# A graph network's first loop: who adds a group's sums to the node table

## The chip, the cores and the metric

The kernel runs on one core of a Trainium2 chip. The metric is the device time of one execution in microseconds. Several runs are made of a kernel and their median is taken.

## The reference, cut to what matters

A graph has 3125 nodes with 64 features and 103125 directed edges (50000 drawn, the same reversed, one loop per node), sorted by destination. Two blocks work on it, each behind a layer norm and a relu, each with a residual. The first (`_L0_gnn_ref`) is two hyperbolic layers on the same graph; the second is a mean over edges of a two-layer perceptron. The part that this change touches is the sum over edges:

```
def hyp_agg(x, src, dst, w, c, n_nodes):
    xt = logmap0(x, c)
    msg = xt[src] * w[:, None]
    agg = jax.ops.segment_sum(msg, dst, num_segments=n_nodes)
    return proj(expmap0(agg, c), c)
```

It is run twice with the same `src`, `dst` and `w`, each time on another `xt`.

## The kernel before, in words

The edges are cut into `NG` = 48 groups of 17 x 128 = 2176. Because they are sorted by destination, the destinations of a group lie in a window of `W` = 72 consecutive nodes; a small table in SBUF (`tabi`) holds where each window begins, and `window(eng, g)` loads that number into a register of the engine that asks.

The first loop builds, for each group, a block matrix of edge weights (source node by destination in the window, 25 blocks of 125 x 72), stores it for the second layer, and applies it to the node table `A` at once. The engines run the loop side by side, each with its own program of bodies, and are tied by counting semaphores (`nth(i)` is the count behind step `i`).

- VectorE (`first_layer`, body for group g): `rank_edges(g+1)` (L1027, reads a PSUM bank), `bucket_edges(g+2)` (L1009), `edge_fields(g+1)` (L1018), `rank_onehots(g+1)` (L1032), `slot_destinations(g)` (L1040), `slot_sources(g)` (L1047), `slot_weights(g)` (three operations, L1055), and from the third body on `add_sums(g-2)` (L1066): it reads the window's place, waits for `applied` and adds the 128 x 72 sums in the bank `agg_ps` to the window of the table `aggTw`. The last two groups are added behind the loop, one on each side of the last apply.
- TensorE (`first_body`): `prefix(g+2)` (L1395 to L1398), `fill_slots(g+1)` (L1407), `first_apply(g-1)` (L1436, 50 small products into `agg_ps`), `slot_rows(g+1)` (L1427), `blocks(g)` (L1419, 75 products in four chunks). `first_apply` waits for the eviction of the block matrix and for `added` of the group before, since there is one bank `agg_ps`.
- ScalarE (`evict`): `third_weights(g)` (L653, 18 operations, waits for `dst1_set` of L1040), `take_slots(g+1)` (L639, L641, L642), `take_rows(g+1)` (L659), and the eviction of the four chunks of blocks (L670).
- SyncE stores the block matrix and the slot rows of each group.
- GpSimd does nothing in this loop. At the head it prepares constants and divides the source indices (L541 to L549) and clears `aggTw`; between the layers it clears two tables; in the last loop (`sum_messages` and its helpers) it subtracts 128 x 512 tiles (L595) beside VectorE.

Behind the loop VectorE waits for the last `added`, answers whether all ranks fit (`answer_ranks`), and folds the table (`act_scales`).

Of the kernel before, what the change touches and what calls it, by code (L numbers as in the profile page):

```python
# [16 lines left out]
NG = -(-E // GE)  # L17
# [43 lines left out]
def gnn_kernel(nc, x, src_t, dst_t, w_t, w0T, b0, w1T, b1, W1, eb1, W2, eb2, out):  # L61
# [5 lines left out]
    with ctx:  # L67
# [72 lines left out]
        def carve(words, dt=f32, parts=128):  # L140
            at[0] += words
            assert at[0] <= ARENA, at[0]
            view = arena[0:parts, at[0] - words:at[0]]
            return view if dt == f32 else view.bitcast(dt)
# [21 lines left out]
        slot_of = carve(NS * GTP // 2, bf16).rearrange("p (s t) -> p s t", t=GTP)  # L166
        minus = carve(64, bf16)[0:1, :]
        third = [carve(NB) for _ in range(2)]
        at[0] = 0
        PQ = carve(NB * HID)[0:PN].rearrange("p (b h) -> p b h", h=HID)  # L170
        P3 = carve(NB * 3 * HID // 2, bf16, PN).rearrange("p (b c h) -> p b c h", c=3, h=HID)
# [90 lines left out]
        def counts(name, n=1):  # L262

            made = [sem(f"{name}{i}") for i in range(n)]
            loop_sems.extend(made)
            return made if n > 1 else made[0]

        def nth(i):

            return i + 1 + PRIMED  # L270
# [5 lines left out]
                                "slots_set"))  # L276
        dst1_set, onehots_set, third_set = counts("dst1_set"), counts("onehots_set"), counts("third_set")
        blocks_done, blocks_set = (counts(n, len(CHUNKS)) for n in ("blocks_done", "blocks_set"))
        applied, added = counts("applied"), counts("added")
        saved = counts("saved")  # L280
        a_stored = sem("a_stored")

# [80 lines left out]
        def in_order(eng, stage):  # L363

            eng.wait_ge(table_set if stage == 0 else ranks_checked, 1)
            return eng.value_load(oki[0:1, stage:stage + 1], min_val=0, max_val=1)
# [145 lines left out]
        def _(pool):  # L512
# [45 lines left out]
            def any_gather(i, table, dest):  # L558
                with pool.Fori(0, NG) as g:
# [7 lines left out]
                    if i == 2:  # L567
                        pool.wait_ge(any_qidx[i], nth(g))
                        pool.sem_inc(begun, 1)
                        for t in range(GT):  # L570
                            pool.indirect_dma_start(GP[1][:, t, :], None, qf_d[:, :],
                                                    bass.IndirectOffsetOnAxis(ap=idx[1][:, t:t + 1], axis=0))\
                                .then_inc(any_gathered_q[i], 16)

            fast = in_order(pool, 1)
            for l in range(2):
                if l == 1:
# [30 lines left out]
        def _(sc):  # L608
# [27 lines left out]
            def take_slots(g, k):  # L636
                sc.wait_ge(slots_done, nth(g))
                sc.wait_ge(onehots_set, nth(g - 2))
                nc.scalar.activation(slot_dst[:, bass.ds(g, 1), :, :].rearrange("p g b d -> p (g b) d"),  # L639
                                     slots_ps[:, 1, 0:NB].unsqueeze(2).broadcast_to([128, NB, 2]), ACT.Copy)  # L640
                nc.scalar.activation(third[k], slots_ps[:, 4, 0:NB], ACT.Copy)  # L641
                nc.scalar.activation(slots[k][:, :, :, :].rearrange("p f b d -> p (f b) d"),  # L642
                                     slots_ps.rearrange("p f b -> p (f b)").unsqueeze(2)
                                     .broadcast_to([128, FIELDS * EB, 2]), ACT.Copy).then_inc(slots_set, 1)
# [11 lines left out]
            def take_rows(g, k):  # L656
                sc.wait_ge(row_done, nth(g))
                sc.wait_ge(row_saved, nth(g - 2))
                nc.scalar.activation(slot_row[k][:, :], row_t_ps, ACT.Copy).then_inc(row_set, 1)  # L659

            def evict(g, k, n):

                third_weights(g, k)
                take_slots(g + 1, 1 - k)
                take_rows(g + 1, 1 - k)
                sc.wait_ge(saved, nth(g - 2))
                sc.wait_ge(applied, nth(g - 2))
                for c, bs in enumerate(CHUNKS):
                    sc.wait_ge(blocks_done[c], nth(g))
                    nc.scalar.activation(AB[k][:, bs[0]:bs[-1] + 1, :], blocks_ps[c], ACT.Copy)\  # L670
                        .then_inc(blocks_set[c], 1)
# [27 lines left out]
            for l in range(2):  # L699
                sc.wait_ge(mu_ps, l + 1)  # L700
                for b in PIECES:
                    square(B[:, b, :], MU[:, b, :])
                answer_tanh()
                answer(ACT.Sqrt)
                answer(ACT.Ln)
                if l == 0:
                    sc.wait_ge(primed, 1)
                    fast = in_order(sc, 0)
                    with sc.If(fast == 1):
                        take_slots(0, 0)  # L710
                        take_rows(0, 0)
                        groups(sc, evict)
                    fast = in_order(sc, 1)

                if l == 0:
                    for c in range(len(QUADS)):
                        sc.wait_ge(fold_set, c + 1)
                        nc.scalar.activation(HT[0:F, QUADS[c][0]:QUADS[c][-1] + 1, :], quad_of(aggTw[0:F, :], c),
                                             ACT.Relu).then_inc(ht_set, 1)
                if l == 1:  # L720
                    square(B[:, :, :], sums_ps[l])
                if l == 1:
                    nc.scalar.activation(C[:, :, :], sums_ps[l], ACT.Relu).then_inc(relu_squared, 1)
                    sc.wait_ge(relu_squared, 1)
                    nc.scalar.activation(C[:, :, :], C[:, :, :], ACT.Square).then_inc(relu_squared, 1)
                answer(ACT.Sqrt)
                if l == 1:
                    answer_tanh()
# [61 lines left out]
        def _(ve):  # L790
# [267 lines left out]
                        slots[k][:, 2 + c, 0:n, :].unsqueeze(2).broadcast_to([128, n, HW, 2]), ALU.mult)  # L1058
                last.then_inc(onehots_set, 1)

            def add_sums(g):
                base = window(ve, g)
                ve.wait_ge(applied, nth(g))
                ve.wait_ge(added, nth(g - 1))
                win = aggTw[:, bass.ds(base, W)]
                nc.vector.tensor_tensor(win, win, agg_ps, ALU.add).then_inc(added, 1)  # L1066

            def ask_ranks():

                ve.tensor_reduce(flag[:, 2:3], rankT, X, ALU.max).then_inc(ranks_max, 1)  # L1070
# [3 lines left out]
            def first_layer():  # L1074

                def body(g, k):
                    rank_edges(g + 1)
                    bucket_edges(g + 2, k)
                    edge_fields(g + 1, 1 - k)
                    rank_onehots(g + 1, 1 - k)  # L1080
                    slot_destinations(g, k)
                    slot_sources(g, k)
                    slot_weights(g, k)
                    if not (isinstance(g, int) and g < 2):
                        add_sums(g - 2)

                bucket_edges(0, 0)
                bucket_edges(1, 1)
                rank_edges(0)
                edge_fields(0, 0)  # L1090
                rank_onehots(0, 0)
                for g in range(3):
                    body(g, g % 2)
                with ve.Fori(0, PAIRS - 1) as j:
                    body(2 * j + 3, 1)
                    body(2 * j + 4, 0)
                if NG % 2 == 0:
                    body(NG - 1, 1)
                ve.wait_ge(rank_set, nth(NG))
                ask_ranks()  # L1100
                add_sums(NG - 2)
                add_sums(NG - 1)
                ve.wait_ge(added, nth(NG - 1))

                ve.wait_ge(prefix_done, nth(NG - 1 + AHEAD))
                ve.wait_ge(slots_done, nth(NG))
# [251 lines left out]
        def _(pe):  # L1358
# [79 lines left out]

            def first_apply(g, k):
                pe.wait_ge(blocks_set[-1], nth(g))  # L1440
                pe.wait_ge(added, nth(g - 1))
                apply(applied, agg_ps, AB[k])

            def sum_flags():
# [191 lines left out]
```

## Time and profile before

| | |
|---|---|
| median of 3 runs | 1189.39 us (1187.72 to 1190.02) |
| profiled execution | 1186.87 us, span 1185.0 us |
| VectorE busy | 1054.7 us, 89% |
| TensorE busy | 1028.0 us, 87% |
| ScalarE busy | 712.7 us, 60% |
| GpSimd busy | 368.7 us, 31% |

A busy share is an average over stages. Durations are those of one profiled execution. The pieces that bear on the change are in the rows below: windows of time, timelines by engine, and single lines with the spread of their durations. In a timeline, the bracket behind a row says how long the engine stood idle before it and which instruction released it; consecutive instructions of one line are merged, and the last number is their count. In all views the first number of a shape is partitions, the second elements of each.

### The profile page before, as it was taken

To read this page: it belongs to the slowest core of one execution; us is meant where nothing else is said; L and a number is where in the kernel's file an instruction comes from. 1 tells how busy PE (TensorE), PEld (TensorE's weight loads), DVE (VectorE), ACT (ScalarE), POOL (GpSimd) and SP (SyncE) were. 2 spreads that over 40 slices of the span, in tenths; PEclk is the share of its full clock that TensorE was granted. 3 is DMA by queue.
4 is the path that set the end of the run, shared out by engine and by line. 5 is a ranking of instruction groups with operands and counts; after the bars stand their busy time and mean duration, and the time that the engine had idled before them with its cause. 6 is when DMAs were issued, how large, how long until landed. Compare 5 with 4: busy or idle time off the path is not lost.

```text
span 1185.0 us, 53692 instructions
## 1 busy us (share of the span) xinstructions
PE 1028.0 (87%) x21722; PEld 951.0 (80%) x21722; DVE 1054.7 (89%) x1448; ACT 712.7 (60%) x1933; POOL 368.7 (31%) x268
## 2 busy tenths in 40 slices
PE   3079898989898998728998599999999999999998
PEld 2058777777787877727998479999999999999997
DVE  8879999999999999785664889999999999999995
ACT  5348888888888888520002576665556555666663
POOL 7000000000000000010000037777777777777774
PEclk9569999999999999759999689999999999999999
DMA  2002323232323232579950255444544445444450
GB/s 82 0 33 100 122 95 126 95 126 95 126 95 126 95 122 99 228 284 337 411 244 18 86 172 164 162 160 152 157 156 159 158 159 161 161 161 161 161 161 29
DMA packets 44877, 169.98 MB, mean 143 GB/s; under 512 B 19440, under 2 KB 19766, under 8 KB 44827
## 3 DMA queue, kind: packets, MB, share of 16 engines
q1 hardware_dynamic: 44827, 169.28, 39.7%
q8 instruction: 36, 0.59, 0.2%
q14 instruction: 14, 0.11, 0.0%
HBM read 121.11 MB, written 48.14 MB: 143 GB/s over the span
## 4 chain that ended last, share of the span: by engine, by line
PE 51%; DVE 32%; issue 9%; DVEq 4%; ACT 2%; DMA 1%; SPq 0%; POOL 0%; ACTq 0%; POOLq 0%
PE PS L1563 17%; PE PS L1565 11%; PE PS L1578 8%; PE PS L1436 8%; DVE arena L1055 7%; DVE arena L1032 5%; DVE arena L1040 4%; DVE arena L1018 3%; PE PS L1583 3%; DVE arena L1027 2%; DVEq L361 2%; PE PS L1467 1%; DMA Cw<-slot_rows 1%; DVE arena L1047 1%; DVE aggTw L1066 1%
## 5 line engine op out<-in xcount | busy, mean ns | idle before, releaser
L595 POOL TENSOR_TENSOR arena<-arena 128x512 bf16<-128x512 f32 x240 | 342.3, 1443 | 319.6 <-ACT arena L773 319.6
L1563 PE MATMUL PS<-arena 125*128 125x128 bf16 x3600 | 344.6, 219 | 2.5 <-DVE HTw L1268 1.0
L773 ACT ACTIVATE arena<-arena 128x512 bf16<-128x512 f32 x240 | 150.8, 628 | 187.1 <-DVE arena L1285 187.1
L1563 PEld LDWEIGHTS PS<-arena 125*128 125x128 bf16 x3600 | 250.4, 97 | 9.3 <-issue 5.1
L1436 PE MATMUL PS<-arena,A 125*64 125x72 f32 x4800 | 179.3, 230 | 65.0 <-DVE aggTw L1066 38.4
L1436 PEld LDWEIGHTS PS<-arena,A 125*64 125x64 f32 x4800 | 165.4, 139 | 74.3 <-issue 49.5
L653 ACT ACTIVATE arena<-arena 128x72 bf16<-128x72 bf16 x864 | 216.9, 344 | 1.7 <-DVE arena L1040 1.7
L1285 DVE SCALAR_TENSOR_TENSOR arena<-PS,arena 128x512 f32<-128x512 f32 x240 | 159.4, 679 | 28.7 <-ACT arena L780 28.7
L780 ACT ACTIVATE arena<-PS 128x512 bf16<-128x512 f32 (+2 forms) x336 | 171.9, 547 | 0.0
L1565 PE MATMUL PS<-arena 108*128 108x128 bf16 x1200 | 167.4, 221 | 0.0
L1565 PE MATMUL PS<-arena,HTw 108*128 108x128 bf16 x1200 | 165.8, 219 | 0.0
L582 POOL MEMSET RT<- 128x3197 f32 x1 | 2.8, 2765 | 476.4 <-PE PS L1512 476.4
L1419 PE MATMUL PS<-arena 128*128 128x72 bf16 x3600 | 127.4, 199 | 0.0
L1419 PEld LDWEIGHTS PS<-arena 128*128 128x128 bf16 x3600 | 121.4, 101 | 4.9
L670 ACT ACTIVATE arena<-PS 128x504 f32<-128x504 f32 x192 | 99.7, 545 | 35.4 <-PE PS L1419 30.6
L1055 DVE TENSOR_TENSOR arena<-arena,slots 128x504 bf16<-128x504 bf16 x144 | 116.0, 855 | 0.0
L1578 PE MATMUL PS<-arena 128*128 128x72 bf16 x2880 | 101.5, 198 | 0.4 <-DVE RT L1322 0.4
L1578 PEld LDWEIGHTS PS<-arena 128*128 128x128 bf16 x2880 | 97.8, 100 | 0.6 <-DVE RT L1322 0.6
L1565 PEld LDWEIGHTS PS<-arena 108*128 108x128 bf16 x1200 | 93.1, 98 | 0.0
L1565 PEld LDWEIGHTS PS<-arena,HTw 108*128 108x128 bf16 x1200 | 92.0, 97 | 0.0
L1264 DVE TENSOR_SCALAR arena<-Bw,colp 125x3200 bf16<-125x3200 bf16 x48 | 81.3, 1693 | 8.1 <-DMA Cw<-slot_rows 7.2
L1398 PE MATMUL PS<-arena,onesb 128*128 128x416 bf16 (+15 forms) x800 | 87.3, 263 | 0.0
(195 smaller groups left out, 1388.5 us busy)
## 6 DMA issues: line engine op xcount, KB each, us to landing
adjacency<-arena SPq DMA_DIRECT2D x48, 900.0 KB, 3.6
arena<-adjacency SPq DMA_DIRECT2D x46, 900.0 KB, 8.0
Bw<-slot_rows SPq DMA_DIRECT2D x48, 800.0 KB, 4.2
Cw<-slot_rows SPq DMA_DIRECT2D x48, 700.0 KB, 4.5
arena<-q_table SPq DMA_DIRECT2D x144, 18.0 KB
q_table<-arena SPq DMA_DIRECT2D x6, 336.0 KB
slot_rows<-slot_row SPq DMA_DIRECT2D x49, 13.0 KB
x_sb<-in_x SPq DMA_DIRECT2D x1, 700.0 KB
```

Source lines behind the costliest of these rows:

```text
L595: nc.gpsimd.tensor_tensor(H3[k][:, at_b, 2, :], Hs[k][:, 4 * q:4 * q + 4, :], H3[k][:, at_b, 1, :], ALU.subtract).then_inc(s_low_set, 1)
L653: last = nc.scalar.activation(WD[k][:, 2, b, :], OD[:, b, :], ACT.Copy, scale=third[k][:, b:b + 1])
L670: nc.scalar.activation(AB[k][:, bs[0]:bs[-1] + 1, :], blocks_ps[c], ACT.Copy)\
L773: nc.scalar.activation(H3[k][:, at_b, 1, :], Hs[k][:, 4 * q:4 * q + 4, :], ACT.Copy).then_inc(s_mid_set, 1)
L780: nc.scalar.activation(whole, ts_ps[q], ACT.Relu).then_inc(s_relu_set, 1)
L1055: last = nc.vector.tensor_tensor(WD[k][:, c, 0:n].rearrange("p b (w d) -> p b w d", d=2), OD[:, 0:n].rearrange("p b (w d) -> p b w d", d=2 ...
L1285: nc.vector.scalar_tensor_tensor(Hs[k][:, 4 * q:4 * q + 4, :], ts_ps[q], 0.0, H3[k][:, at_b, 0, :], ALU.max, ALU.subtract).then_inc(s_rest ...
L1419: last = mm(blocks_ps[c][:, i, :], OS[k][:, b, :], WD[k][:, part, b, :], start=(part == 0), stop=(part == 2))
L1436: last = mm(sums[half, :], A[:, b, :], adjacency[0:PN, b, :], start=(b < 2), stop=(b >= NB - 2))
L1563: mm(ps, OTs[k][:, b, :], P3[:, b, part, :], start=(part == 0), stop=False)
L1565: last = mm(ps, OTd[k][a][:, b, :], qs[k][:, a, :], start=False, stop=(a == 1))
L1578: mm(rs_ps, H3[k][:, b, part, :], OB[k][:, b, :], start=(b == 0 and part == 0), stop=False)
```

## The change

Two tiles of 128 x 72 (`taken`) are new. ScalarE copies the sums of group g-1 from the bank into one of them in its body for group g, between `take_slots` and `take_rows` (`take_sums`), once more behind the loop for the last group, and counts `sums_taken`. TensorE's `first_apply` waits for `sums_taken` of the group before instead of `added`. GpSimd gets a loop over the groups (`groups(pool, add_sums)`), in which it loads the window's place, waits for `sums_taken`, and adds the tile to the table. VectorE's `add_sums` is gone from the bodies and from behind the loop; its last wait for `added` stays.

```
--- before.py
+++ after.py
@@ -166,6 +166,7 @@
         slot_of = carve(NS * GTP // 2, bf16).rearrange("p (s t) -> p s t", t=GTP)
         minus = carve(64, bf16)[0:1, :]
         third = [carve(NB) for _ in range(2)]
+        taken = [carve(W) for _ in range(2)]
         at[0] = 0
         PQ = carve(NB * HID)[0:PN].rearrange("p (b h) -> p b h", h=HID)
         P3 = carve(NB * 3 * HID // 2, bf16, PN).rearrange("p (b c h) -> p b c h", c=3, h=HID)
@@ -276,7 +277,7 @@
                                 "slots_set"))
         dst1_set, onehots_set, third_set = counts("dst1_set"), counts("onehots_set"), counts("third_set")
         blocks_done, blocks_set = (counts(n, len(CHUNKS)) for n in ("blocks_done", "blocks_set"))
-        applied, added = counts("applied"), counts("added")
+        applied, sums_taken, added = counts("applied"), counts("sums_taken"), counts("added")
         saved = counts("saved")
         a_stored = sem("a_stored")
 
@@ -572,6 +573,18 @@
                                                     bass.IndirectOffsetOnAxis(ap=idx[1][:, t:t + 1], axis=0))\
                                 .then_inc(any_gathered_q[i], 16)
 
+            def add_sums(g, k, n):
+
+                base = window(pool, g)
+                pool.wait_ge(sums_taken, nth(g))
+                pool.wait_ge(added, nth(g - 1))
+                win = aggTw[:, bass.ds(base, W)]
+                nc.gpsimd.tensor_tensor(win, win, taken[k], ALU.add).then_inc(added, 1)
+
+            fast = in_order(pool, 0)
+            with pool.If(fast == 1):
+                pool.wait_ge(agg_cleared, 1)
+                groups(pool, add_sums)
             fast = in_order(pool, 1)
             for l in range(2):
                 if l == 1:
@@ -658,10 +671,17 @@
                 sc.wait_ge(row_saved, nth(g - 2))
                 nc.scalar.activation(slot_row[k][:, :], row_t_ps, ACT.Copy).then_inc(row_set, 1)
 
+            def take_sums(g, k):
+                sc.wait_ge(applied, nth(g))
+                sc.wait_ge(added, nth(g - 2))
+                nc.scalar.activation(taken[k], agg_ps, ACT.Copy).then_inc(sums_taken, 1)
+
             def evict(g, k, n):
 
                 third_weights(g, k)
                 take_slots(g + 1, 1 - k)
+                if not (isinstance(g, int) and g == 0):
+                    take_sums(g - 1, 1 - k)
                 take_rows(g + 1, 1 - k)
                 sc.wait_ge(saved, nth(g - 2))
                 sc.wait_ge(applied, nth(g - 2))
@@ -710,6 +730,7 @@
                         take_slots(0, 0)
                         take_rows(0, 0)
                         groups(sc, evict)
+                        take_sums(NG - 1, (NG - 1) % 2)
                     fast = in_order(sc, 1)
 
                 if l == 0:
@@ -1058,13 +1079,6 @@
                         slots[k][:, 2 + c, 0:n, :].unsqueeze(2).broadcast_to([128, n, HW, 2]), ALU.mult)
                 last.then_inc(onehots_set, 1)
 
-            def add_sums(g):
-                base = window(ve, g)
-                ve.wait_ge(applied, nth(g))
-                ve.wait_ge(added, nth(g - 1))
-                win = aggTw[:, bass.ds(base, W)]
-                nc.vector.tensor_tensor(win, win, agg_ps, ALU.add).then_inc(added, 1)
-
             def ask_ranks():
 
                 ve.tensor_reduce(flag[:, 2:3], rankT, X, ALU.max).then_inc(ranks_max, 1)
@@ -1081,8 +1095,6 @@
                     slot_destinations(g, k)
                     slot_sources(g, k)
                     slot_weights(g, k)
-                    if not (isinstance(g, int) and g < 2):
-                        add_sums(g - 2)
 
                 bucket_edges(0, 0)
                 bucket_edges(1, 1)
@@ -1098,8 +1110,6 @@
                     body(NG - 1, 1)
                 ve.wait_ge(rank_set, nth(NG))
                 ask_ranks()
-                add_sums(NG - 2)
-                add_sums(NG - 1)
                 ve.wait_ge(added, nth(NG - 1))
 
                 ve.wait_ge(prefix_done, nth(NG - 1 + AHEAD))
@@ -1438,7 +1448,7 @@
 
             def first_apply(g, k):
                 pe.wait_ge(blocks_set[-1], nth(g))
-                pe.wait_ge(added, nth(g - 1))
+                pe.wait_ge(sums_taken, nth(g - 1))
                 apply(applied, agg_ps, AB[k])
 
             def sum_flags():
```

## Rows read from the trace of the kernel before

**Rows 1.** Windows of two single bodies: each engine's busy time (instructions), clock, DMA
```profile
core 0: us, PE busy (x) PEld busy (x) DVE busy (x) ACT busy (x) POOL busy (x), PEclk, DMA share, GB/s
...
77.87:86.27 8.40, 7.30 (x98) 6.25 (x99) 8.40 (x10) 5.44 (x20) 0.00 (x0) 0.63 0.14 57
86.27:94.81 8.54, 8.33 (x174) 7.32 (x172) 8.54 (x11) 7.51 (x29) 0.00 (x0) 1.00 0.31 120
```

**Rows 2.** Timeline of VectorE in the loop: start, duration, line, operation, count
```profile
300.55 1.29 DVE L1018 TENSOR_TENSOR arena<-arena 128x2210 bf16<-128x2210 bf16 x1
301.77 1.34 DVE L1032 TENSOR_TENSOR arena<-arena 128x2304 bf16<-128x2304 bf16 x1
303.04 1.07 DVE L1040 TENSOR_TENSOR arena<-ramp1b,slots 128x1800 bf16<-128x1800 bf16 x1
...
305.78 2.41 DVE L1055 TENSOR_TENSOR arena<-arena,slots 128x504 bf16<-128x504 bf16 x3
308.12 0.21 DVE L1066 TENSOR_TENSOR aggTw<-aggTw,PS 128x72 f32 x1
308.26 0.60 DVE L1027 TENSOR_REDUCE arena<-PS 128x442 f32 x1
```

**Rows 3.** Part 5 of the page: line, shapes, count; busy us, mean ns; idle before
```profile
L1436 PE MATMUL PS<-arena,A 125*64 125x72 f32 x4800 | 179.3, 230 | 65.0 <-DVE aggTw L1066 38.4
```

**Rows 4.** Timeline of TensorE over the same body
```profile
306.34 1.25 PE L1407 MATMUL PS<-arena 128*128 128x130 bf16 x17
308.39 1.84 PE L1436 MATMUL PS<-arena,A 125*64 125x72 f32 x50 [0.80 <-DVE aggTw L1066]
310.06 0.22 PE L1427 MATMUL PS<-identb,slots 128*52 128x128 bf16 x1
```

**Rows 5.** Timeline of ScalarE over the same body
```profile
304.84 4.52 ACT L653 ACTIVATE arena<-arena 128x72 bf16<-128x72 bf16 x18
309.26 0.19 ACT L639 ACTIVATE slot_dst<-PS 128x50 f32 x1
...
309.43 0.37 ACT L642 ACTIVATE slots<-PS 128x260 bf16<-128x260 f32 x1
310.32 0.27 ACT L659 ACTIVATE slot_row<-PS 52x128 bf16<-52x128 f32 x1 [0.52 <-PE PS L1427]
311.19 2.17 ACT L670 ACTIVATE arena<-PS 128x504 f32<-128x504 f32 x4 [0.60 <-PE PS L1419]
313.25 4.51 ACT L653 ACTIVATE arena<-arena 128x72 bf16<-128x72 bf16 x18
```

**Rows 6.** VectorE's L1278 by its line: duration in ns, min/median/max
```profile
L1278 DVE TENSOR_TENSOR arena<-ramp,slot_dst x48: 524/1490/1498, 690.6 to 1163.1; 128x360 f32<-128x360 f32 x48
```

**Rows 7.** Timeline of GpSimd in the last loop
```profile
802.57 1.85 POOL L595 TENSOR_TENSOR arena<-arena 128x512 bf16<-128x512 f32 x1
```

**Rows 8.** Timeline of VectorE around it
```profile
802.51 0.90 DVE L1275 TENSOR_TENSOR arena<-ramp1b,slot_dst 128x1440 bf16<-128x1440 bf16 x1
803.32 1.49 DVE L1278 TENSOR_TENSOR arena<-ramp,slot_dst 128x360 f32<-128x360 f32 x1
804.74 0.22 DVE L1322 TENSOR_TENSOR RT<-RT,PS 128x72 f32 x1
```

**Rows 9.** GpSimd's L595 by its line, columns as in Rows 6
```profile
L595 POOL TENSOR_TENSOR arena<-arena x240: 1157/1445/1858, 698.2 to 1170.6; 128x512 bf16<-128x512 f32 x120
```

**Rows 10.** Timeline at the head of the kernel, GpSimd and VectorE
```profile
17.12 2.18 POOL L549 TENSOR_TENSOR arena<-arena 128x850 f32<-128x850 f32 x1
...
17.61 2.31 DVE L871 SCALAR_TENSOR_TENSOR A<-A,rows 125x576 f32<-125x576 f32 x1
```

**Rows 11.** Lines by form, VectorE behind 650 us: L871 on 576 columns
```profile
L871 DVE SCALAR_TENSOR_TENSOR A<-A,rows 125x576 f32<-125x576 f32 x1 | 0.8, 758 | 0.1
```

**Rows 12.** Lines by form, GpSimd: an instruction on one column
```profile
L516 POOL IOTA colpi<- 128x1 int32 x1 | 0.1, 136 | 0.0
```

**Rows 13.** Timeline at the loop's end: the last apply
```profile
484.24 1.84 PE L1436 MATMUL PS<-arena,A 125*64 125x72 f32 x50 [0.40 <-ACT arena L670]
```

More of the change, by code:

```diff
@@ L168, in gnn_kernel @@
         third = [carve(NB) for _ in range(2)]
+        taken = [carve(W) for _ in range(2)]
         at[0] = 0
@@ L278, in gnn_kernel @@
         blocks_done, blocks_set = (counts(n, len(CHUNKS)) for n in ("blocks_done", "blocks_set"))
-        applied, added = counts("applied"), counts("added")
+        applied, sums_taken, added = counts("applied"), counts("sums_taken"), counts("added")
         saved = counts("saved")
@@ L573, in any_gather, with add_sums @@
                                 .then_inc(any_gathered_q[i], 16)
+            def add_sums(g, k, n):
+                base = window(pool, g)
+                pool.wait_ge(sums_taken, nth(g))
+                pool.wait_ge(added, nth(g - 1))
+                win = aggTw[:, bass.ds(base, W)]
+                nc.gpsimd.tensor_tensor(win, win, taken[k], ALU.add).then_inc(added, 1)
+            fast = in_order(pool, 0)
+            with pool.If(fast == 1):
+                pool.wait_ge(agg_cleared, 1)
+                groups(pool, add_sums)
             fast = in_order(pool, 1)
@@ L659, in take_rows, with take_sums @@
                 nc.scalar.activation(slot_row[k][:, :], row_t_ps, ACT.Copy).then_inc(row_set, 1)
+            def take_sums(g, k):
+                sc.wait_ge(applied, nth(g))
+                sc.wait_ge(added, nth(g - 2))
+                nc.scalar.activation(taken[k], agg_ps, ACT.Copy).then_inc(sums_taken, 1)
             def evict(g, k, n):
@@ L664, in evict @@
                 take_slots(g + 1, 1 - k)
+                if not (isinstance(g, int) and g == 0):
+                    take_sums(g - 1, 1 - k)
                 take_rows(g + 1, 1 - k)
@@ L712, in _ @@
                         groups(sc, evict)
+                        take_sums(NG - 1, (NG - 1) % 2)
                     fast = in_order(sc, 1)
@@ L1059, in slot_weights @@
                 last.then_inc(onehots_set, 1)
[L1061 to L1066, printed above, removed]
             def ask_ranks():
@@ L1083, in body @@
                     slot_weights(g, k)
-                    if not (isinstance(g, int) and g < 2):
-                        add_sums(g - 2)
                 bucket_edges(0, 0)
@@ L1100, in first_layer @@
                 ask_ranks()
-                add_sums(NG - 2)
-                add_sums(NG - 1)
                 ve.wait_ge(added, nth(NG - 1))
@@ L1440, in first_apply @@
                 pe.wait_ge(blocks_set[-1], nth(g))
-                pe.wait_ge(added, nth(g - 1))
+                pe.wait_ge(sums_taken, nth(g - 1))
                 apply(applied, agg_ps, AB[k])
```

## The prediction, made before the kernel ran

> **What bounds the kernel now.** I read the page's engine shares first (VectorE 89%, TensorE 87%), then the windows of single bodies of the first loop, then the timelines of VectorE, TensorE and ScalarE over one body, and last the places of the later stages where GpSimd and VectorE work at the same time. In the windows the reader is to see that VectorE is busy for every microsecond of both bodies: 8.40 of 8.40 us in the body for group 1, which has no `add_sums`, and 8.54 of 8.54 us in the body for group 2, the first one that has it [rows 1]. In VectorE's timeline each instruction starts before its forerunner ends, with no gap anywhere: L1066, the add, starts at 308.12 and the next body's L1027 at 308.26 [rows 2]. VectorE sets the pace of the loop; the other two follow.
>
> The page tempts one to another reading: L1436, `first_apply` on TensorE, idles 38.4 us for VectorE's add [rows 3]. That idle time is TensorE's slack in a loop that it does not bound, so its removal is worth nothing in the loop's body, and something only at the tail.
>
> **Removed from VectorE.** 46 adds stand in bodies (groups 2 to 47 each add the sums of the group two before), two behind the loop. One costs not its 0.21 us but what it pushes the next start back: 308.26 - 308.12 = 0.14 us [rows 2], and 8.54 - 8.40 = 0.14 us by the windows [rows 1]. Credit: 46 x 0.14 = 6.4 us, if nothing else slows VectorE.
>
> **TensorE's wait moved** from `added` to `sums_taken`. `first_apply` could start when `fill_slots` (L1407) ends, 306.34 + 1.25 = 307.59, instead of at 308.39 [rows 4]. `sums_taken` of the group before is signalled most of a body earlier. The apply then lasts 1.84 us, to about 309.4. The next instruction, L1427 at 310.06 [rows 4], now waits for ScalarE's `slots_set`, the end of L642 at 309.43 + 0.37 = 309.80 [rows 5]; it can start near 309.85, 0.2 us sooner.
>
> **Added to ScalarE:** one copy of 128x72 out of the bank per group. The nearest rows are 0.19 us for 50 columns (L639) and 0.37 us for 260 (L642) [rows 5]; I take 0.21 us, bounds 0.19 and 0.37. It stands between L642 and L659, where ScalarE idles 0.52 us for TensorE's L1427 [rows 5]. L1427 would end near 309.85 + 0.22 = 310.07 and the copy near 309.73 + 0.21 = 309.94, so the copy is covered; uncovered it would cost ScalarE its 0.21 us. The ScalarE-TensorE loop without VectorE's hold is: L653's start to L642's end 4.96, 0.05 to L1427, L1427 to L670 1.13, L670 to the next L653 2.06 [rows 4, 5], together 8.20 us, and 8.41 us even with the copy uncovered. That is VectorE's new pace at worst. Its own waits behind the copy: `applied`, over by about 309.4, and `added` of two groups before, long over. Queued behind it are `take_rows` and the evictions, which TensorE's next apply and the store need; the store has a body of time. ScalarE will therefore run ahead until `third_weights` meets `dst1_set`, the end of L1040 at 304.11, against 304.84 now [rows 2, 5]: up to 0.7 us ahead of today's phase.
>
> **Added to GpSimd:** a register load, two waits and a 72-column add of two SBUF inputs per group, on an engine with no other work in this loop. Its own time is hidden. What counts is what it does to VectorE. The profile shows that these two engines shut each other out. L1278, an operation of VectorE with two SBUF inputs, takes 0.524 us when GpSimd is idle and 1.490 us in nearly all of its 48 executions [rows 6]. Around one of them: a GpSimd L595 starts at 802.57 and lasts 1.85 us instead of 1.16 while L1275 is running, and L1275 itself is not lengthened; the following L1278 then is, by 0.97 us [rows 7 to 9]. So GpSimd waits for the running VectorE operation, goes next, and VectorE's next two-input operation waits until GpSimd has read. L1322, with one input in PSUM, keeps 0.22 us beside it [rows 8].
>
> In the first loop every operation of a body but L1027 (its input is in PSUM) reads two SBUF tensors. Where will GpSimd ask? ScalarE's copy ends about 5.2 us behind L1040's end (0.05 + 4.96 + 0.14), GpSimd asks 0.1 us later, that is near 304.11 + 5.3 = 309.4 in today's times. The next body's L1027 starts at 308.26, its L1018 one body after 300.55, at 309.09, and L1032 at 310.31 [rows 2]. The request falls into L1018; GpSimd goes at its end, and L1032 waits. If ScalarE did not run ahead, the copy would end at 309.94, in L1018 still.
>
> **The price of one such stop, h.** No row shows a 72-column add on GpSimd. In proportion to L1278: 0.966 x 72 / 512 = 0.136 us. From the head of the kernel: L871 takes 2.31 us behind L549, an f32 add of 850 columns, instead of 0.758 [rows 10, 11], so 1.55 us, and at most 2.04 us if counted from L549's start at 17.12; times 72/850 that is 0.13 to 0.17. Upper bound: a fixed part as long as a one-column instruction of GpSimd, 0.136 us [rows 12], on top: 0.27 us. Lower bound: of L595's 1.157 us [rows 9] 0.19 lie outside the stop of 0.966; an add of 0.136 + 72 x (1.157 - 0.136) / 512 = 0.28 us would stop VectorE for 0.09. I take 0.14 us, the proportion, which lies near both operations measured. Net over the bodies: 46 x (0.14 - 0.14) = 0; bounds 46 x (0.09 - 0.14) = -2.3 and 46 x (0.27 - 0.14) = +6.0 us.
>
> By the Trainium skill, "SBUF — State Buffer", section "Who interferes with whom", a VectorE instruction with two SBUF inputs contends with a GpSimd instruction that reads SBUF, and whichever starts first keeps the shared pair while the other is fully blocked. By that rule this change pays back what it takes off VectorE; the trace agrees, with 0.97 us on L1278 [rows 6, 8]. The same skill, "GPSIMD Engine Reference", section "Performance pitfalls for Q7 kernels", gives about 102 cycles for each read command that is not overlapped; at its 1.2 GHz two of them are 0.17 us, and with the columns above h would be an estimated 0.31, the bodies +8 us and the time 1196 us. No row here shows that part by itself.
>
> **The tail.** The last apply starts at 484.24, released by ScalarE's eviction L670 [rows 13]. With ScalarE up to 0.7 us and L1427 0.2 us earlier it starts about 0.9 us earlier. Behind it now stand a copy (0.21), GpSimd's add (0.28 by the line above) and a second signal (about 0.1) instead of one VectorE add (0.21): +0.4. Net -0.5 us, between -1.0 and +0.5.
>
> **Sum.** Against the profiled execution: 1186.87 (its span of 1185.0 and 1.87 around it) + 0 - 0.5 = 1186.4. That execution lies 2.5 us below the median of 1189.39; on the median's level the forecast is 1188.9 us.
>
> **Rivals.**
> *GpSimd's stop is longer than the add it replaces.* Place: L1032 in each of 46 bodies; price h - 0.14. It decides for slower by over 2.4 us (0.2% of the time, about what a measurement of this kernel tells from no change) from h = 0.14 + 2.9/46 = 0.20. For it: any fixed part at all on top of the proportion, and the upper bound of 0.27. Against: the two measured stops, at 512 and 850 columns, leave no clear fixed part. With h = 0.24: +4.6 - 0.5, 1193.5 us.
> *The add finds a free place,* beside L1027 or because VectorE's queued operation goes first. Then the full credit stands: -6.4 - 0.5, 1182.5 us. Against it: the request comes some 1.1 us behind L1027's start, and GpSimd got its turn in front of nearly every L1278 [rows 2, 6].
> *The stop is shorter than the proportion,* 0.09 or less: about -2.8, 1186.6 us.
> *ScalarE becomes the bound,* if copy, both signals and the wait for TensorE do not overlap as worked out: two uncovered parts of 0.25 us over 8.20 give 8.70, or 46 x 0.16 - 0.5 = +6.9, 1196.3 us. Against: 0.52 and 0.60 us of idle time in each body [rows 5].
>
> **Chances and range.** Forecast 0.42; longer stop 0.28; free place 0.12; shorter stop 0.13; ScalarE 0.05. The first lies within 0.2%, the second and last are slower (0.33), the third and fourth faster (0.25). The forecast's own range is 1186.5 to 1191.3. The range of 8 in 10 takes the shorter stop and most of the longer: 1184.5 to 1194.5, leaving out the free place and ScalarE.
>
> **What would show it.** Right: L1032 lasts longer by h in each body (1.48 us where it was 1.34), all other VectorE operations as before; the body's period stays 8.54; GpSimd's add begins while L1018 runs and shows more than its own 0.3 us, because it waits; L1436 no longer waits for VectorE; the copy fits before L659. Wrong: L1032 unchanged and a period of 8.40 (free place); a period above 8.60 with L1032 longer by over 0.2 (longer stop); idle time on VectorE ahead of L1040 for ScalarE (ScalarE bound).

## The result, and the profile after

| | before | after |
|---|---|---|
| median of 6 runs | 1188.52 us (1187.11 to 1190.02) | 1183.07 us (1180.62 to 1184.12) |
| ratio | | 0.9952, 95% interval 0.9939 to 0.9964 |
| profiled execution, span | 1186.87, 1185.0 us | 1182.70, 1181.0 us |

The change makes the kernel faster, by 5.4 us between the medians and by 0.48% as the ratio of the runs has it. The forecast was 1188.9 us, no change; the time lies below its range.

In the page of the changed kernel GpSimd is the surprise: its 48 adds (L582 here) are busy for 318 us, 6.6 us each, most of the first loop. TensorE no longer waits for an add (L1446, which was L1436). Columns as in [rows 3].

```profile
PE 1032.8 (87%) x21722; PEld 951.6 (81%) x21722; DVE 1050.3 (89%) x1400; ACT 720.7 (61%) x1981; POOL 687.1 (58%) x317
...
L582 POOL TENSOR_TENSOR aggTw<-aggTw,arena 128x72 f32 x48 | 318.2, 6630 | 132.2 <-ACT arena L677 132.2
...
L1446 PE MATMUL PS<-arena,A 125*64 125x72 f32 x4800 | 179.0, 229 | 29.2 <-DVE A L957 25.7
```

Windows of single bodies of the changed kernel, the counterparts of [rows 1]: the first two are the bodies of groups 1 and 2, the third one from the middle of the loop. All three now take 8.40 us, and VectorE is still busy throughout.

```profile
77.74:86.14 8.40, 7.30 (x101) 6.43 (x102) 8.40 (x11) 5.43 (x20) 0.00 (x0) 0.65 0.13 55
86.14:94.54 8.40, 8.01 (x169) 7.00 (x168) 8.40 (x11) 7.48 (x29) 5.16 (x1) 1.00 0.29 112
305.14:313.54 8.40, 7.75 (x161) 6.75 (x161) 8.40 (x11) 7.48 (x29) 7.24 (x1) 1.00 0.28 111
```

VectorE's timeline over one body, the counterpart of [rows 2]. The line numbers have moved: L1048 is `rank_edges` (was L1027), L1030 `bucket_edges` (L1009), L1039 `edge_fields` (L1018), L1053 `rank_onehots` (L1032), L1061 `slot_destinations` (L1040), L1068 `slot_sources` (L1047), L1076 `slot_weights` (L1055).

```profile
305.43 1.30 DVE L1039 TENSOR_TENSOR arena<-arena 128x2210 bf16<-128x2210 bf16 x1
306.65 1.35 DVE L1053 TENSOR_TENSOR arena<-arena 128x2304 bf16<-128x2304 bf16 x1
307.92 1.08 DVE L1061 TENSOR_TENSOR arena<-ramp1b,slots 128x1800 bf16<-128x1800 bf16 x1
...
310.66 2.42 DVE L1076 TENSOR_TENSOR arena<-arena,slots 128x504 bf16<-128x504 bf16 x3
313.01 0.61 DVE L1048 TENSOR_REDUCE arena<-PS 128x442 f32 x1
313.54 0.37 DVE L1030 TENSOR_TENSOR arena<-rampb,arena 128x442 bf16<-128x442 bf16 x1
313.83 1.30 DVE L1039 TENSOR_TENSOR arena<-arena 128x2210 bf16<-128x2210 bf16 x1
```

GpSimd's timeline over the same body:

```profile
306.02 7.24 POOL L582 TENSOR_TENSOR aggTw<-aggTw,arena 128x72 f32 x1 [1.14 <-ACT arena L677]
314.41 7.27 POOL L582 TENSOR_TENSOR aggTw<-aggTw,arena 128x72 f32 x1 [1.15 <-ACT arena L677]
```

The add begins at 306.02, in the middle of L1039, as forecast. But L1053 behind it keeps its 1.35 us, and so does every other operation. The add ends only at 306.02 + 7.24 = 313.26, 0.25 us behind the start of L1048, the one operation of the body that does not read two SBUF tensors. GpSimd was shut out at six changes of operation (from L1039 to L1053, L1061, L1068 and the three of L1076), then worked beside L1048, where it costs nothing.

TensorE and ScalarE over the same body, against [rows 4] and [rows 5] (L1417, L1446, L1437 were L1407, L1436, L1427; L655, L672, L690 were L642, L659, L670; the copy is L677):

```profile
302.05 1.26 PE L1417 MATMUL PS<-arena 128*128 128x130 bf16 x17
303.24 1.84 PE L1446 MATMUL PS<-arena,A 125*64 125x72 f32 x50
305.79 0.24 PE L1437 MATMUL PS<-identb,slots 128*52 128x128 bf16 x1 [0.71 <-ACT slots L655]
```

```profile
305.36 0.37 ACT L655 ACTIVATE slots<-PS 128x260 bf16<-128x260 f32 x1
305.63 0.22 ACT L677 ACTIVATE arena<-PS 128x72 f32<-128x72 f32 x1
306.07 0.27 ACT L672 ACTIVATE slot_row<-PS 52x128 bf16<-52x128 f32 x1 [0.22 <-PE PS L1437]
306.94 2.17 ACT L690 ACTIVATE arena<-PS 128x504 f32<-128x504 f32 x4 [0.60 <-PE PS L1429]
```

The apply follows `fill_slots` without a gap, L1437 now waits for ScalarE, and the copy (0.22 us; forecast 0.21) fits into ScalarE's wait for L1437, of which 0.22 us are left.

The end of the loop, before and after. VectorE's next operation behind the last add, at 486.90 and at 480.08, serves as a mark:

```profile
486.22 0.23 DVE L1066 TENSOR_TENSOR aggTw<-aggTw,PS 128x72 f32 x1 [4.80 <-PE PS L1436]
486.90 0.16 DVE L1190 TENSOR_SCALAR flag<-PS 128x1 f32<-128x1 f32 x1 [0.45 <-DVE aggTw L1066]
```

```profile
477.04 1.84 PE L1446 MATMUL PS<-arena,A 125*64 125x72 f32 x50 [0.40 <-ACT arena L690]
...
478.91 0.23 ACT L677 ACTIVATE arena<-PS 128x72 f32<-128x72 f32 x1 [1.93 <-PE PS L1446]
479.31 0.31 POOL L582 TENSOR_TENSOR aggTw<-aggTw,arena 128x72 f32 x1 [5.11 <-ACT arena L677]
480.08 0.16 DVE L1200 TENSOR_SCALAR flag<-PS 128x1 f32<-128x1 f32 x1 [6.25 <-POOL aggTw L582]
```

Up to the mark the changed kernel gains 486.90 - 480.08 = 6.8 us. VectorE's last `rank_edges` stands at 470.49 before and 464.17 after, so 6.3 us come from the bodies and 0.5 from the tail (16.4 us before, 15.9 after). Behind the mark this execution takes 2.8 us longer (1181.0 - 480.1 = 700.9 against 1185.0 - 486.9 = 698.1). The change does nothing there, and the run below that gives the add back to VectorE took 701.5 us for the same part. In the other runs with one add a group this part takes 699.0 to 703.5 us, so 698.1 lies at the low end of a spread of some 5 us; its cause is open. A second spread lies at the loop's entry: VectorE's second `rank_edges` starts about 3.1 us behind the first in some executions and 4.9 in others, whatever the kernel (4.9 in both of these). The 5.4 us between the medians and the 6.8 us up to the mark differ by less than these spreads.

### The profile page after: what moved, and what is told of

It reads as the page before. It is cut to its first block, busy times and chain, and to the rows that moved or that the text cites. A ratio compares the mean times of both kernels' runs of the same rounds, so it can differ in the third digit from the quotient of the medians.

```text
span 1181.0 us, 53889 instructions
## 1 busy us (share of the span) xinstructions
PE 1032.8 (87%) x21722; PEld 951.6 (81%) x21722; DVE 1050.3 (89%) x1400; ACT 720.7 (61%) x1981; POOL 687.1 (58%) x317
## 4 chain that ended last, share of the span: by engine, by line
PE 61%; DVE 18%; ACT 12%; issue 6%; DMA 1%; DVEq 1%; POOL 1%; ACTq 0%; SPq 0%; POOLq 0%
PE PS L1573 18%; PE PS L1575 12%; ACT arena L666 8%; PE PS L1588 8%; PE PS L1446 8%; PE PS L1429 5%; PE PS L1593 3%; DVE arena L1076 3%; PE PS L1408 3%; DVE arena L1053 2%; DVE arena L1061 2%; DVE arena L1039 1%; DVE arena L1048 1%; PE PS L1477 1%; PE PS L1555 1%
## 5 line engine op out<-in xcount | busy, mean ns | idle before, releaser
L582 POOL TENSOR_TENSOR aggTw<-aggTw,arena 128x72 f32 x48 | 318.2, 6630 | 132.2 <-ACT arena L677 132.2
L1446 PE MATMUL PS<-arena,A 125*64 125x72 f32 x4800 | 179.0, 229 | 29.2 <-DVE A L957 25.7
L1446 PEld LDWEIGHTS PS<-arena,A 125*64 125x64 f32 x4800 | 164.4, 138 | 36.1 <-issue 28.0
L690 ACT ACTIVATE arena<-PS 128x504 f32<-128x504 f32 x192 | 99.6, 544 | 35.6 <-PE PS L1429 30.6
L1076 DVE TENSOR_TENSOR arena<-arena,slots 128x504 bf16<-128x504 bf16 x144 | 116.1, 857 | 0.0
```

What stands on the lines that cost most here:

```text
L582: nc.gpsimd.tensor_tensor(win, win, taken[k], ALU.add).then_inc(added, 1)
L1076: last = nc.vector.tensor_tensor(WD[k][:, c, 0:n].rearrange("p b (w d) -> p b w d", d=2), OD[:, 0:n].rearrange("p b (w d) -> p b w d", d=2 ...
L1446: last = mm(sums[half, :], A[:, b, :], adjacency[0:PN, b, :], start=(b < 2), stop=(b >= NB - 2))
```

## The experiments

All edits are made to the changed kernel. Where only the profile mattered there was one execution. Each ratio is to runs of the kernel before that were made together with it.

**VectorE adds ScalarE's copy.** GpSimd's loop is left out.

```
+            def add_sums(g, k):        # VectorE, at its old place, and twice behind the loop
+                base = window(ve, g)
+                ve.wait_ge(sums_taken, nth(g))
+                ve.wait_ge(added, nth(g - 1))
+                win = aggTw[:, bass.ds(base, W)]
+                nc.vector.tensor_tensor(win, win, taken[k], ALU.add).then_inc(added, 1)
```

> ScalarE copies the sums as in the changed kernel and TensorE waits for the copy, but VectorE does the add, at its old place, from the copy; GpSimd does nothing in the loop. Theory (the whole gain is VectorE's add taken off its path, about 46 x 0.14 us): body period 8.54 us again and a time like that of the kernel before, within 2 us (ratio 0.998 to 1.001), the rest being the tail. Rival (the gain comes from TensorE's freed wait and ScalarE running ahead): the gain of 5 us stays, ratio about 0.995.

Measured: ratio to before 1.0003 (0.9991 to 1.0015). VectorE's timeline has the 0.15 us of the add and a period of 314.92 - 306.38 = 8.54 us:

```profile
306.23 0.22 DVE L1075 TENSOR_TENSOR aggTw<-aggTw,arena 128x72 f32 x1
306.38 0.61 DVE L1036 TENSOR_REDUCE arena<-PS 128x442 f32 x1
...
314.92 0.61 DVE L1036 TENSOR_REDUCE arena<-PS 128x442 f32 x1
```

TensorE's freed wait and ScalarE's lead are worth nothing by themselves; the gain is VectorE's add leaving its path.

**An idle operation in the add's place.** VectorE does a maximum over 72 columns, one SBUF input, at the end of each body from the third on. Scratch tiles are cleared before the loop here and in its four relatives below.

```
+            def extra():
+                nc.vector.tensor_reduce(scr[0][:, 0:1], scr[1], X, ALU.max)
```

> The changed kernel with one idle operation of VectorE (a maximum over 72 columns, one SBUF input, about 0.14 to 0.2 us of pace) at the old place of the add; its result is used nowhere. Theory (VectorE's pace is all): period 8.54 to 8.56 us, the time back to within 2 us of the kernel before. GpSimd's add, which I now think gets to SBUF only when VectorE runs an operation that does not read two SBUF tensors, ends some 0.1 to 0.2 us earlier relative to L1048's start, beside the idle operation. Rival (VectorE is not what the gain came from): ratio 0.995 as without it.

Measured: ratio 1.0018 (1.0005 to 1.0030), period 8.53 to 8.54 us. The gain is gone, from the other side. GpSimd's add ended at 315.29 with the idle operation begun at 315.04 and L1048's counterpart at 315.18: it used the new opening. The ratio here, and in the two experiments below whose operation stands in the middle and has 72 columns, lies 0.2 to 0.3% above 1 although the period is that of the kernel before; what makes up that part is not shown.

**The same operation in the middle of the body,** between `edge_fields` and `rank_onehots`.

> The same idle one-input operation, but in the middle of VectorE's body, behind edge_fields (L1039) and ahead of rank_onehots (L1053), where GpSimd's request has just arrived. Theory A (GpSimd is held off until VectorE starts an operation that does not read two SBUF tensors): GpSimd's add now ends right behind this operation, after about 1 us instead of 7.2 us, and what is left of its stop falls on L1053 (h minus the cover of 0.14 us: 0 to 0.1 us); period 8.54 to 8.65. Theory B (GpSimd waits about 7 us by some ageing whatever VectorE runs): the add still takes 7.2 us.

Measured: period 8.54 us, ratio 1.0026 (1.0014 to 1.0038). VectorE (L1090 the idle operation, L1054 `rank_onehots`) and GpSimd (L583 the add):

```profile
310.86 0.21 DVE L1090 TENSOR_REDUCE arena<-arena 128x1 f32<-128x72 f32 x1
311.00 1.34 DVE L1054 TENSOR_TENSOR arena<-arena 128x2304 bf16<-128x2304 bf16 x1
```

```profile
310.24 0.88 POOL L583 TENSOR_TENSOR aggTw<-aggTw,arena 128x72 f32 x1 [7.64 <-ACT arena L678]
```

The add takes 0.88 us instead of 7.24: it ends at 311.12, 0.26 us behind the idle operation's start, just as it did behind L1048's. Of the 46 adds in bodies 44 end so, 0.24 to 0.28 us behind the start of the idle operation; the first two asked behind it. Ageing (theory B) is out. L1054 keeps its 1.34 us, so the 0.14 us of the idle operation cover the whole stop.

**The shortest opening,** the same with two columns instead of 72.

> As the run with a one-input operation in the middle of VectorE's body, but over two columns instead of 72, so that the opening is as short as an operation can be (about 0.06 us of pace). If GpSimd gets in by it, the add ends within about 1 us and L1053 behind it is longer by what is left of the stop, 0.05 to 0.1 us; that gives h, together with the 0.14 us that the 72-column operation hid in full. If so short an operation gives no opening, the add ends behind L1048 as in the changed kernel.

Measured, VectorE's timeline (L1049 `rank_edges`):

```profile
299.78 0.61 DVE L1049 TENSOR_REDUCE arena<-PS 128x442 f32 x1
...
301.83 0.14 DVE L1090 TENSOR_REDUCE arena<-arena 128x1 f32<-128x2 f32 x1
301.89 1.42 DVE L1054 TENSOR_TENSOR arena<-arena 128x2304 bf16<-128x2304 bf16 x1
...
308.32 0.61 DVE L1049 TENSOR_REDUCE arena<-PS 128x442 f32 x1
```

The idle operation pushes L1054 back by 301.89 - 301.83 = 0.06 us and L1054 lasts 1.42 instead of 1.34 us. So h = 0.06 + 0.08 = 0.14 us, and the period, 308.32 - 299.78 = 8.54, is 8.40 + h. GpSimd's add took 0.91 us.

**A two-input f32 operation there,** `nc.vector.tensor_tensor(scr[0], scr[1], scr[2], ALU.add)`.

> At the same place in the middle an f32 add of two SBUF tensors of 72 columns (result used nowhere). All other two-input operations of this loop are bf16. Theory A: no opening, GpSimd's add still takes 7.2 us and ends behind L1048; period 8.40 + 0.14 = 8.54. Rival C (GpSimd gets its turn where VectorE changes from a bf16 to an f32 operation, as ahead of L1278 in the last loop): the add ends after about 1 us, the f32 operation itself or the next is lengthened by h = 0.1 to 0.25 us, period 8.65 to 8.8.

Measured: ratio 1.0017 (1.0007 to 1.0028), period 8.54; VectorE (L1090 the f32 operation), then GpSimd:

```profile
302.20 0.23 DVE L1090 TENSOR_TENSOR arena<-arena 128x72 f32<-128x72 f32 x1
302.35 1.35 DVE L1054 TENSOR_TENSOR arena<-arena 128x2304 bf16<-128x2304 bf16 x1
```

```profile
301.57 7.42 POOL L583 TENSOR_TENSOR aggTw<-aggTw,arena 128x72 f32 x1 [1.15 <-ACT arena L678]
```

No opening, no operation lengthened: two SBUF inputs shut GpSimd out in f32 as in bf16.

**One shaped like L1278 of the kernel before.** L1278 was what the forecast took its rule from.

```
+                five = [128, 5, W]
+                nc.vector.tensor_tensor(Cw[:, 0:5 * W].rearrange("p (b w) -> p b w", w=W),
+                                        ramp[:, 1:1 + W].unsqueeze(1).broadcast_to(five),
+                                        scr[1].bitcast(bf16)[:, 0:10].rearrange("p (b d) -> p b d", d=2)[:, :, 0]
+                                        .unsqueeze(2).broadcast_to(five), ALU.is_equal)
```

> An idle operation of the shape of L1278 of the kernel before (five blocks of 72, an f32 input repeated over blocks and a bf16 input repeated over columns, f32 out) in the middle of VectorE's body of the first loop. Rival C (it is this kind of operation ahead of which GpSimd gets its turn): GpSimd's add ends within about 1 us and this operation or the next is 0.14 us longer than the 0.52 us it takes alone. Theory D (the moment of the request decides, not the kind): the add is held off and ends behind L1048 as before, 7.6 us.

Measured: 1202.0 us in the one execution, the period 8.84 us (the 0.44 us by which the operation pushes the next start back, on top of 8.40). The operation takes 0.54 us, nothing is lengthened, the add takes 7.7 us and ends behind L1048's counterpart. Rival C is out in this loop.

**The two one-hots of the last loop exchanged.**

> In the last loop VectorE's two one-hot operations change places: the f32 one (0.52 us alone) first, the bf16 one (0.90) second. GpSimd's subtraction asks near the start of the first of them. Rival C: the f32 one is still the one that is lengthened by about 0.97 us, though it comes first. Theory D or any theory by order: the first keeps its 0.52 us and the second, bf16, is lengthened, to 1.5 to 1.9 us.

Measured, VectorE's timeline in the last loop (L1285 the f32 one, L1288 the bf16 one):

```profile
807.84 0.52 DVE L1285 TENSOR_TENSOR arena<-ramp,slot_dst 128x360 f32<-128x360 f32 x1
808.28 1.87 DVE L1288 TENSOR_TENSOR arena<-ramp1b,slot_dst 128x1440 bf16<-128x1440 bf16 x1
```

The f32 operation has its 0.52 us, the bf16 one is lengthened from 0.90 to 1.87, again by 0.97 us; over the whole loop the first takes 0.52 to 0.53 us and the second has a median of 1.87. The time of the one execution is 1182.05 us, as without the exchange. The place in the order decides, not the kind.

**The copy at other moments.** Behind ScalarE's 4th third_weights operation, behind the 2nd, at the end of its body, and behind `take_rows`; and, by counts of a semaphore on GpSimd, two moments shortly before a change of operation.

```
+                        if b == CB - 1 + 4 and from_third(g):     # the 4th; 2 for the 2nd
+                            take_sums(g - 2, k)
```

> ScalarE copies the sums behind the 4th of its 18 third_weights operations, so that GpSimd's add asks about 4.5 us later than in the changed kernel, near 0.2 us before VectorE's L1068 gives way to L1076. In the changed kernel one add out of 48, at 97.66 us, came about 0.2 us before a change of operation, got through between two operations with two SBUF inputs, lasted 0.46 us and lengthened L1061 from 1.08 to 1.22 us. Theory D (a request that meets the change of operation gets in, one that comes in the middle of an operation is held off until the opening at L1048): many adds last 0.3 to 0.6 us, and L1076's first part is 0.14 us longer in those bodies; with all of them caught the period is 8.54 and the gain of the change is gone (ratio near 1.000). Rival A (only the opening counts): every add ends behind L1048, 2.7 us after it began; period 8.40, ratio 0.995.

> As the run with the copy behind the 4th third_weights operation, but behind the 2nd: GpSimd asks 0.5 us earlier, near the middle of VectorE's L1068 (some 0.7 us before its end). Theory D: every add is held off and ends behind L1048, after some 3.2 us; period 8.40, ratio 0.995 as in the changed kernel. Rival (any request late in the body gets in somewhere among the three parts of L1076): stops of 0.14 us, period 8.54, ratio 1.000.

> ScalarE copies the sums at the end of its body, behind the eviction. GpSimd asks about 3.4 us later than in the changed kernel, 0.3 to 0.6 us behind L1068's start. Theories A and D: the add still ends behind L1048 and lasts about 3.8 us instead of 7.2, period 8.40. Theory B (ageing of about 7 us): it ends somewhere in the next body.

> ScalarE copies the sums behind take_rows, so that GpSimd's lone request comes some 0.64 us later than in the changed kernel, within 0.1 us of the change from L1039 to L1053. Theory D (the moment decides; a request at the change gets in): many adds last 0.3 to 1.7 us and L1053 or L1061 is 0.14 us longer in those bodies. Theory E (only a GpSimd instruction directly behind another gets in, whatever its moment): all adds last about 6.6 us and end behind L1048; period 8.40.

> GpSimd counts up an unused semaphore 4 times (even groups) or 6 times (odd groups) between its waits and its add, which delays the lone request by an estimated 0.3 and 0.5 us (some 60 such counts took 4.99 us at the head of the kernel), to about 0.4 and 0.2 us before the change from L1039 to L1053. The one add that got in by itself came 0.19 us before the next operation's start. Theory D: the adds of one parity at least get in, last about 0.5 us, and L1053 is 0.14 us longer there. Theory E: all adds last about 6.8 us.

Measured: with the 4th, ratio 0.9951 (0.9930 to 0.9973), with the 2nd 0.9980 (0.9966 to 0.9994), the other three had one execution each (1183.61, 1180.90 and 1181.21 us). The median durations of the add were 1.02, 2.11, 2.95, 6.65 and 6.79 us, each reaching from another moment of asking to the same opening, and VectorE's period was 8.40 us in all five. In the traces of the late copies, c7 and c8 VectorE's operations show up to 0.06 us more than in the changed kernel, and overlap by as much; the period does not move. (The smaller gain with the 2nd is not the period's. The late copies lengthen the tail: from the last `rank_edges` to the mark it takes 17.5 us with the 2nd and 18.0 with the 4th, against 15.9 in the changed kernel.) The request of the first came not where I had aimed it but some 0.7 us before `rank_edges`. That of c7 met the change of operation exactly (304.79, when L1053 starts), those of c8 came 0.14 and 0.27 us before it. c7, GpSimd and VectorE:

```profile
304.79 6.63 POOL L582 TENSOR_TENSOR aggTw<-aggTw,arena 128x72 f32 x1 [1.75 <-ACT arena L677]
```

```profile
304.79 1.38 DVE L1053 TENSOR_TENSOR arena<-arena 128x2304 bf16<-128x2304 bf16 x1
...
311.14 0.64 DVE L1048 TENSOR_REDUCE arena<-PS 128x442 f32 x1
```

Theory D falls: a request at or just ahead of a change of operation is held off as well. But three adds did get in. One is in the changed kernel, its second (VectorE, then GpSimd):

```profile
96.58 1.35 DVE L1053 TENSOR_TENSOR arena<-arena 128x2304 bf16<-128x2304 bf16 x1
97.85 1.22 DVE L1061 TENSOR_TENSOR arena<-ramp1b,slots 128x1800 bf16<-128x1800 bf16 x1
```

```profile
97.66 0.46 POOL L582 TENSOR_TENSOR aggTw<-aggTw,arena 128x72 f32 x1 [2.85 <-ACT arena L677]
```

L1061 lasts 1.22 instead of 1.08 us, h = 0.14 again. The other two are also second adds: at 96.44 us in c8, with 0.14 us more on the operation behind it, and at 101.20 us in b4, where the add took 1.14 us and the last part of L1076 1.23 instead of 1.09. All three fall where VectorE and GpSimd enter their loops, but in c4, whose first loop is that of the changed kernel, the second add is held off like the others. The changed kernel and the nine runs that give GpSimd one add a body and no opening in the middle have 460 adds in bodies; 457 end 0.25 to 0.33 us behind the start of L1048's counterpart (or of the idle operation next to it), and these three end before it. What makes them exceptions stays open.

**A long operation of GpSimd in the opening.** A subtraction of 512 columns, result used nowhere, behind each add. Its tile is cleared before the loop, and VectorE waits for the last subtraction behind it; these lines are left out here.

```
+                pool.wait_ge(extra_set, g + 1)
+                nc.gpsimd.tensor_tensor(RT[:, 0:256].bitcast(bf16), RT[:, 512:1024], RT[:, 1024:1536], ALU.subtract)\
+                    .then_inc(extra_set, 1)
```

> GpSimd does a subtraction of 512 columns (f32 in, bf16 out, result used nowhere) behind each add, so that both meet the opening at L1048 (0.53 us of pace). Theory (what GpSimd has begun in the opening is not cut short, and stops VectorE's next operation with two SBUF inputs): L1030 is longer by 0.6 to 0.8 us and the period is 9.0 to 9.2 us. Rival (openings end when VectorE wants the port back): L1030 unchanged, period 8.40.

Measured, in one execution: 1233.64 us, 46 more than the runs of before made with it. The mean period is 9.46 us, where 9.0 to 9.2 were expected. VectorE (L1054 `rank_edges`, then L1036, L1045, L1059) and GpSimd (L585 the subtraction, L583 the add):

```profile
302.05 0.61 DVE L1054 TENSOR_REDUCE arena<-PS 128x442 f32 x1
302.58 1.19 DVE L1036 TENSOR_TENSOR arena<-rampb,arena 128x442 bf16<-128x442 bf16 x1
303.69 1.44 DVE L1045 TENSOR_TENSOR arena<-arena 128x2210 bf16<-128x2210 bf16 x1
305.06 2.42 DVE L1059 TENSOR_TENSOR arena<-arena 128x2304 bf16<-128x2304 bf16 x1
```

```profile
302.26 1.26 POOL L585 TENSOR_TENSOR RT<-RT 128x512 bf16<-128x512 f32 x1
303.49 0.48 POOL L583 TENSOR_TENSOR aggTw<-aggTw,arena 128x72 f32 x1
303.93 2.34 POOL L585 TENSOR_TENSOR RT<-RT 128x512 bf16<-128x512 f32 x1
```

The first subtraction, begun in the opening, holds up L1036: 1.19 us instead of 0.37, 0.82 more. Then it goes on: the next add follows GpSimd's last instruction directly, gets in at the very next change and costs L1045 0.14 us (1.44 instead of 1.30), and the next subtraction costs L1059 1.07 us (2.42 instead of 1.35), though L1045 and L1059 have two SBUF inputs each. This is the pattern of L1278 in the last loop, where three L595 follow each other: GpSimd gets its turn at a change of operation.

It tempts one to the rule that an instruction directly behind another takes turns and a lone one is shut out. The same trace speaks against it. In its bodies 10 adds follow a subtraction directly and 9 begin 1.0 to 1.35 us behind one, and all 19 get in. Of the 27 that begin 6.4 us behind or later, 20 are held off and 7 get in. Two of these, and VectorE's next operation behind the start of each:

```profile
247.02 0.90 POOL L583 TENSOR_TENSOR aggTw<-aggTw,arena 128x72 f32 x1 [6.37 <-ACT arena L683]
295.08 7.22 POOL L583 TENSOR_TENSOR aggTw<-aggTw,arena 128x72 f32 x1 [6.38 <-ACT arena L683]
```

```profile
247.64 1.49 DVE L1059 TENSOR_TENSOR arena<-arena 128x2304 bf16<-128x2304 bf16 x1
...
295.70 1.35 DVE L1059 TENSOR_TENSOR arena<-arena 128x2304 bf16<-128x2304 bf16 x1
```

Both asked 0.62 us before the change to L1059, 6.4 us behind GpSimd's last instruction. The first got in there and cost L1059 0.14 us, the second waited for the opening. Sixteen adds of this run asked like these two, 0.58 to 0.63 us before that change: 7 got in, 9 did not. So neither the moment nor the distance from GpSimd's last instruction decides by itself; what does, the runs do not show.

## Why the prediction was wrong

- *Credit of 46 x 0.14 = 6.4 us:* right. The bodies gained 6.3 us, with one stop of 0.14 in them, and the two runs that gave VectorE an operation back lost it all.
- *TensorE's wait is slack, worth nothing in the bodies:* right; with that part alone the ratio is 1.0003.
- *ScalarE's copy is covered:* right, 0.22 us, and ScalarE stays off the path.
- *GpSimd asks during L1039 (then L1018):* right, 0.59 us behind its start.
- *h = 0.14 us:* right wherever a stop happened (L1061 at 97.85, the two-column run, the adds behind a subtraction).
- *"GpSimd goes at its end, and L1032 waits":* this is the step that failed. It went into the sum as 46 x 0.14 us, and was paid once: of the 46 requests in bodies one got in between two operations with two SBUF inputs, and 45 were held off until L1048, the operation without two SBUF inputs. The rule was read off L1278, where GpSimd's instruction followed another of its own. That this difference is what matters is not shown; the run with the subtraction has adds far behind GpSimd's last instruction that got in at a change, and paid. The rival "free place" had this mechanism and the time (1182.5 us, measured 1183.07), at a chance of 0.12; I set it low because nearly all 48 L1278 spoke against it, and all of these were one and the same situation.
- *Tail -0.5 us:* right, 16.4 to 15.9 us.
- *The Trainium skill,* "SBUF — State Buffer", section "Who interferes with whom", says that the one to issue first holds the shared pair for the whole instruction. That GpSimd is fully blocked is what the trace shows. Measured, the block lasts not for one instruction (the longest has 1.8 us) but for the chain, 7 us. The 1196 us that the same paragraph of the prediction names for an h of 0.31 us is 1188.9 + 8 = 1196.9 by its own sum, and the measured h of 0.14 us shows no such extra part.

## What to carry to other kernels

Work moved from a bounding VectorE to an idle GpSimd can be free, even between operations with two SBUF inputs. Here it was, because nearly every request was held off until an operation with an input in PSUM that is longer than GpSimd's stop, and because nobody needs GpSimd's result before that. The add waited 7 us of an 8.4 us body. This is no rule to count on: with a second GpSimd instruction in each body the time was 46 us above that of the kernel before, and adds that asked at the same moment were partly held off and partly let in. Look in the new trace at which operations of VectorE are longer than before. Before taking a rule on contention from one place of a trace, ask in how many different situations it was seen there, and look for the price (here 0.14 us a stop) and for how often it is paid as two separate numbers.

## What the runs showed of the hardware that was not expected

- In the ten runs with one GpSimd add a body and no opening in the middle, 457 of 460 adds of 0.31 us ended only behind the first VectorE operation with one input, 0.25 to 0.33 us behind its start. A gapless chain of operations with two SBUF inputs, bf16 or f32, held them off for up to 7.7 us. An operation with one input in SBUF that pushed the next one back by only 0.06 us was enough to let an add in. All operations that let one in here were reductions (`tensor_reduce`), from PSUM or from SBUF; other kinds were not tried.
- With a subtraction behind each add, 26 of 46 adds got in between two VectorE operations with two SBUF inputs, at a stop of 0.14 us for 72 columns. A subtraction of 512 columns cost 1.07 us between two such operations, and 0.82 where it had begun 0.32 us earlier in the opening. The stop is nearly proportional to the columns.
